# A new timetable for a fused Mamba and MoE layer: where the conv taps, the transposed B and the output projections stand

## The reference

```python
def layer(x):                       # x: 8 x 1024 x 256, fp32
    x = x + mamba(layernorm(x))
    return x + moe(layernorm(x))

def mamba(x):                       # ED = 512 channels, N = 16 states, R = 64
    xp, z = split(x @ in_proj_w.T)
    xc = silu(causal_conv(xp, conv_w, taps=4))          # per channel
    dt, B, C = split(xc @ x_proj_w.T)                   # 64, 16, 16
    delta = softplus(dt @ dt_proj_w.T + dt_proj_b)
    h[t] = exp(delta[t] * A) * h[t-1] + delta[t] * B[t] * xc[t]     # 512 x 16 states
    y = sum_n(h * C) + D * xc
    return (y * silu(z)) @ out_proj_w.T

def moe(x):                         # squared-relu expert; routed experts weigh in by trunc(softmax(top 2))
    return relu(x @ Ws1)**2 @ Ws2 + routed(x)
```

## Time and profile before

| | |
|---|---|
| median of 3 runs | 1702.7 us (1702.11 to 1709.6) |
| the profiled execution | 1708.5 us, its span 1706.6 us |
| busy: DVE, PE, POOL, ACT | 1546.8, 1474.5, 1373.7, 1260.4 us |
| scans (L851), 1024 of them | 613.4 and 582.6 us busy |
| products by C on POOL (L1120), 512 | 1207.4 us busy |
| DMAs of a chunk, 512 KB, median from issue to landing | x 3.8 to 3.9 us, out 2.9 us |

### The profile page before, as it was taken

How to read it: one execution, slowest core, us unless ns; L and a number is a source line. 1 busy time by engine, 2 the same in 40 slices (tenths; PEclk the granted TensorE clock), 3 DMA queues, 4 the chain that set the end, 5 groups by cost and what they waited for, 6 DMA issues and landing times.

```text
span 1706.6 us, 38017 instructions
## 1 busy us (share of the span) xinstructions
PE 1474.5 (86%) x15138; PEld 1129.3 (66%) x15138; DVE 1546.8 (91%) x1833; ACT 1260.4 (74%) x2053; POOL 1373.7 (80%) x991
## 2 busy tenths in 40 slices
PE   7788989888899888988889988898989888898776
PEld 4556666666766666766666766666667666667665
DVE  4888999999999999999999899999989989998885
ACT  5877677887777778787777877788677777777651
POOL 1788788887879788897888878888787987879783
PEclk9999999999999999999999999999999999999999
DMA  4103021130302203031030301203031120302101
GB/s 141 61 2 124 1 100 51 39 113 2 124 26 79 73 14 137 2 112 38 39 112 2 137 13 70 82 15 137 2 112 39 39 99 2 113 25 87 64 14 39
DMA packets 45863, 105.89 MB, mean 62 GB/s; under 512 B 9649, under 2 KB 35121, under 8 KB 37490
## 3 DMA queue, kind: packets, MB, share of 16 engines
q1 hardware_dynamic: 45682, 103.42, 17.2%
HBM read 86.10 MB, written 17.30 MB: 61 GB/s over the span
## 4 chain that ended last, share of the span: by engine, by line
DVE 34%; PE 31%; ACT 18%; issue 13%; POOL 1%; DVEq 1%; SPq 1%; DMA 0%; ACTq 0%; POOLq 0%
DVE hs L851 29%; ACT da L542 10%; PE BX L215 10%; PE PA L257 4%; PE Y L237 4%; PE PA L282 2%; DVE PA L881 2%; PE PB L330 2%; PE PB L282 1%; PE PB L305 1%; PE PB L347 1%; ACT xp L575 1%; PE PA L291 1%; ACT xc L646 1%; PE PB L339 1%
## 5 line engine op out<-in xcount | busy, mean ns | idle before, releaser
L1120 POOL TENSOR_TENSOR hs<-hs,cb 128x1024 f32<-128x1024 f32 x512 | 1207.4, 2365 | 183.3 <-DVE hs L851 162.0
L542 ACT ACTIVATE da<-delta,a_neg 128x512 f32<-128x512 f32 x1024 | 667.6, 711 | 83.4 <-DVE hs L851 82.4
L851 DVE TENSOR_TENSOR_SCAN hs<-da,hlast,BX 128x512 f32<-128x512 f32 x512 | 613.4, 1261 | 56.5 <-PE BX L215 55.6
L851 DVE TENSOR_TENSOR_SCAN hs<-da,BX 128x512 f32<-128x512 f32 x512 | 582.6, 1201 | 52.1 <-PE BX L215 51.0
L237 PEld LDWEIGHTS Y<-ident,hs 128*128 128x128 f32 x4096 | 471.3, 142 | 98.1 <-issue 71.0
L237 PE MATMUL Y<-ident,hs 128*128 128x128 f32 x4096 | 523.8, 275 | 5.4 <-POOL hs L1120 5.3
L215 PE MATMUL BX<-bd,uT 32*128 32x128 f32 x8192 | 302.9, 284 | 155.0 <-DVE hs L851 152.6
L215 PEld LDWEIGHTS BX<-bd,uT 32*128 32x128 f32 x8192 | 253.7, 187 | 214.0 <-DVE hs L851 208.1
L575 ACT ACTIVATE xp<-PA 128x512 f32<-128x512 f32 x60 | 35.9, 598 | 125.9 <-PE PA L257 125.9
L257 PE MATMUL PA<-xnT,w_in 128*128 128x512 f32 x240 | 120.8, 626 | 4.2 <-ACT gate L600 3.4
L1116 POOL COPY hlast<-hs 128x2 f32<-128x2 f32 x256 | 47.9, 187 | 90.2 <-DVE hs L851 90.0
(11 more groups left out here) (169 smaller groups left out, 1467.2 us busy)
## 6 DMA issues: line engine op xcount, KB each, us to landing
cb<-c_scratch SPq DMA_DIRECT2D x64, 1024.0 KB, 4.6
x<-in_x SPq DMA_DIRECT2D x16, 512.0 KB, 3.8
x_scratch<-x2T SPq DMA_DIRECT2D x16, 512.0 KB, 2.6
xt<-in_x SPq DMA_DIRECT2D x15, 512.0 KB, 3.9
out<-x SPq DMA_DIRECT2D x15, 512.0 KB, 2.9
w_in<-in_in_wT SPq DMA_DIRECT2D x1, 1024.0 KB, 10.3
c_scratch<-dbc SPq DMA_DIRECT2D x64, 8.0 KB, 1.5
x2n<-in_x SPq DMA_DIRECT2D x1, 512.0 KB, 4.9
```

Of the source, the lines that this page charges most:

```text
L542: e.activation(da[:, k % DR, q, :], delta[:, g, :], ACT.Exp, scale=a_neg[:, g, n:n + 1]).then_inc(s_da, 1)
L851: e.tensor_tensor_scan(hs[:, k % HR, q, :], da[:, k % DR, q, :], BX[:, :].rearrange("p (t n) -> p n t", n=RT)[:, n % RT, :], hlast[:, g, n ...
L1120: e.tensor_tensor(hs[:, k % HR, :, :], hs[:, k % HR, :, :], cb[:, Q * p:Q * p + Q, :], ALU.mult).then_inc(s_hc, 1)
```

## The change

All five orders and the two bank tables are rewritten. The conv of chunk c+1 begins with group 0 at step 28 of chunk c-1 and goes on at steps 0, 4 and 8; its taps on VectorE are split over odd steps 29/31, 1, 5/7 and 9/11. `act_bt` copies the transposed B from PA to a new SBUF tile `bt`, and `dve_bd` reads it there; the four bd stand at steps 21, 23, 23 and 25. `pe_out` computes tiles in halves, and the second residual tile pair goes through PA. `pe_z(3)` moves to step 1 of the next chunk, `pe_dt(2)` to 8, `pe_ut` and `pe_yt` move, `pool_rstd2` to step 18, `sp_x` to step 6. Waits and semaphores follow the new banks. What is computed stays. The diff, with the removed lines of the orders left out:

```diff
@@ -14,12 +14,12 @@
 EXPS = "natural_log_exp_and_others"
 
 
-BANK_A = {0: [("xp", 1, 0)], 2: [("trc", 2, 1)], 3: [("o", -2, 1)], 4: [("xp", 1, 1)], 7: [("z", 1, 0)],
-          8: [("xp", 1, 2)], 12: [("xp", 1, 3)], 16: [("dbc", 1, 0)], 20: [("bt", 1, 0)], 24: [("z", 1, 2)],
-          26: [("ut", 1, 0)], 28: [("yt", 0, 0)], 29: [("yt", 0, 1)], 30: [("z", 1, 3)]}
-BANK_B = {1: [("trc", 2, 0)], 2: [("o", -2, 0)], 4: [("ut", 0, 1)], 5: [("yt", -1, 3)], 6: [("dt", 0, 2)],
-          9: [("ut", 0, 2)], 10: [("res", -1, 0)], 14: [("res", -1, 1)], 16: [("dt", 0, 3)], 19: [("ut", 0, 3)],
-          20: [("dt", 1, 0)], 22: [("z", 1, 1), ("otr", -1, 0)], 23: [("otr", -1, 1)], 24: [("hl", -1, 0), ("trc0", 2, 0)],
+BANK_A = {0: [("xp0", 1, 0), ("xp", 1, 1)], 2: [("o", -2, 0)], 4: [("xp0", 1, 1), ("xp", 1, 2)],
+          8: [("xp0", 1, 2), ("xp", 1, 3)], 12: [("xp0", 1, 3), ("ut", 0, 2)], 13: [("res", -1, 1)], 16: [("dbc", 1, 0)],
+          20: [("bt", 1, 0), ("yt", 0, 0)], 22: [("z", 1, 1)], 24: [("z", 1, 2)], 26: [("ut", 1, 0)], 27: [("yt", 0, 1)], 28: [("xp", 2, 0)]}
+BANK_B = {1: [("z", 0, 3)], 2: [("ut", 0, 1)], 3: [("o", -2, 1)], 4: [("trc", 2, 0)], 5: [("trc", 2, 1)], 6: [("yt", -1, 3)],
+          7: [("z", 1, 0)], 8: [("dt", 0, 2)], 10: [("res", -1, 0)], 16: [("dt", 0, 3)], 19: [("ut", 0, 3)],
+          20: [("dt", 1, 0)], 22: [("otr", -1, 0)], 23: [("otr", -1, 1)], 24: [("hl", -1, 0), ("trc0", 2, 0)],
           26: [("hl", -1, 1), ("trc0", 2, 1)], 28: [("ht", -1, 0)], 29: [("yt", 0, 2)], 30: [("dt", 1, 1)]}
 
 
@@ -29,10 +29,13 @@
     for c in range(n_chunks):
         for s in range(steps):
             for stage, off, i in places.get(s, ()):
-                if stage in ("trc", "trc0"):
-                    if (stage == "trc0") != (c == 0):
-                        continue
-                    stage = "trc"
+                if stage in ("trc", "trc0") and (stage == "trc0") != (c == 0):
+                    continue
+                if stage in ("xp", "xp0") and (stage == "xp0") != (c == 0) and (c, off) != (0, 2):
+                    continue
+                if (stage, c + off) == ("z", 0):
+                    continue
+                stage = stage.rstrip("0")
                 if 0 <= c + off < n_chunks and (stage, c + off, i) not in at:
                     at[stage, c + off, i] = len(at)
...
@@ -321,16 +325,18 @@
                 mm = e.transpose(bank[:, t * P:(t + 1) * P], gate[c % 2][:, t, g * P:(g + 1) * P], ident[:, :])
             mm.then_inc(done, 1)
 
-        def pe_out(e, c, t, part=0):
+        def pe_out(e, c, t, lo=0, hi=G):
             kk, t2 = divmod(t, 2)
-            if t2 == 0:
-                e.wait_ge(s_pb_out, max(b_use["res", c, kk], b_use["yt", c, G - 1] + 1))
+            bank, n, done, out = bank_of("res", c, kk)
+            if t2 == 0 and lo == 0:
+                e.wait_ge(out, n)
+                e.wait_ge(s_pb_out, b_use["yt", c, G - 1] + 1)
                 e.wait_ge(s_pa_out, a_use["yt", c, 1] + 1)
-            for g in range(part * G // 2, G if part or t != 1 else G // 2):
-                mm = e.matmul(PB[:, t2 * DM:(t2 + 1) * DM], ygT[:, g, t * P:(t + 1) * P], w_out[:, g, :],
+            for g in range(lo, hi):
+                mm = e.matmul(bank[:, t2 * DM:(t2 + 1) * DM], ygT[:, g, t * P:(t + 1) * P], w_out[:, g, :],
                               start=(g == 0), stop=(g == G - 1))
-            if t == 3 or part:
-                mm.then_inc(s_pb, 1)
+            if t2 and hi == G:
+                mm.then_inc(done, 1)
...
@@ -410,71 +416,78 @@
             for c in range(NQ):
                 for s in range(S):
                     k = S * c + s
+                    if on(c):
+                        if s == 2:
+                            pe_ut(e, c, 1)
+                        if s == 8:
+                            pe_dt(e, c, 2)
+                        if s == 16:
+                            pe_dt(e, c, 3)
+                        if s % NP == 2:
+                            pe_skip(e, c, s // NP)
+                    if c == 0 and s in (0, 4, 8, 12):
+                        pe_xp(e, 1, s // 4)
+                    if c and on(c + 1) and s in (0, 4, 8):
+                        pe_xp(e, c + 1, s // 4 + 1)
+                    if s == 12:
+                        pe_ut(e, c, 2)
+                    if s == 28 and on(c - 1):
+                        pe_htr(e, c - 1)
+                    if s == 28 and on(c + 2):
+                        pe_xp(e, c + 2, 0)
+                    if s == 1 and c:
+                        pe_z(e, c, 3)
+                    if s in (2, 3) and on(c - 2):
+                        pe_shared(e, c - 2, s - 2)
+                    if s in (4, 5) and c and on(c + 2):
+                        pe_trc(e, c + 2, s - 4)
+                    if s in (24, 26) and c == 0:
+                        pe_trc(e, 2, s // 2 - 12)
+                    if on(c - 1):
+                        if s == 6:
+                            pe_yt(e, c - 1, 3)
+                        if s == 10:
+                            pe_out(e, c - 1, 0)
+                        if s == 11:
+                            pe_out(e, c - 1, 1, 0, G // 2)
+                        if s == 12:
+                            pe_out(e, c - 1, 1, G // 2, G)
+                        if s == 13:
+                            pe_out(e, c - 1, 2, 0, G // 2)
+                        if s == 14:
+                            pe_out(e, c - 1, 2, G // 2, G)
+                        if s == 15:
+                            pe_out(e, c - 1, 3)
+                        if s == 23:
+                            pe_otr(e, c - 1, 1)
+                        if s in (24, 26):
+                            pe_hidden(e, c - 1, s // 2 - 12)
                     if on(c + 1):
                         if s in (16, 18):
                             pe_dbc(e, c + 1, s // 2 - 8)
                         if s == 20:
                             pe_bt(e, c + 1)
                             pe_dt(e, c + 1, 0)
+                        if s == 7:
+                            pe_z(e, c + 1, 0)
+                        if s in (22, 24):
+                            pe_z(e, c + 1, s // 2 - 10)
                         if s == 26:
                             pe_ut(e, c + 1, 0)
                         if s == 30:
                             pe_dt(e, c + 1, 1)
                     if s == 22 and on(c - 1):
                         pe_otr(e, c - 1, 0)
+                    if s == 19:
+                        pe_ut(e, c, 3)
+                    if s == 20:
+                        pe_yt(e, c, 0)
+                    if k >= 2:
+                        pe_sum(e, k - 2)
+                    if s == 27:
+                        pe_yt(e, c, 1)
+                    if s == 29:
+                        pe_yt(e, c, 2)
                     if s % 2 and 0 <= k + 1 < S * NQ:
                         pe_bx(e, (k + 1) // 2)
...
+        def act_bt(e, c):
+            e.wait_ge(s_pa, a_use["bt", c, 0] + 1)
+            e.wait_ge(s_bd, NR * c)
+            e.activation(bt[:, :, :], PA[:, 0:J * FX].rearrange("p (j f) -> p j f", j=J)[:, :, R:R + N],
+                         ACT.Copy).then_inc(s_pa_out, 1)
...
@@ -732,83 +755,87 @@
             for c in range(NQ):
                 for s in range(S):
                     k = S * c + s
+                    if c == 0 and s == 0:
+                        act_halo(e, 1)
+                    if c == 0 and s in (0, 4, 8, 12):
+                        act_xp(e, 1, s // 4)
+                    if c and on(c + 1) and s in (0, 4):
+                        act_xp(e, c + 1, s // 4 + 1)
+                    if s == 2:
                         act_ut(e, c, 1)
+                    if s == 3:
+                        act_silu_z(e, c)
+                    if s in (4, 5) and c and on(c + 2):
+                        act_trc(e, c + 2, s - 4)
+                    if s == 6 and on(c - 1):
+                        act_yt(e, c - 1, 3)
+                    if s == 8:
+                        act_softplus(e, c, 2)
+                        if c and on(c + 1):
+                            act_xp(e, c + 1, 3)
+                    if s == 12:
+                        act_ut(e, c, 2)
+                    if s == 16:
+                        act_softplus(e, c, 3)
+                    if s == 20 and on(c + 1):
+                        act_bt(e, c + 1)
+                        act_softplus(e, c + 1, 0)
+                    if s == 21 and on(c - 1):
+                        act_norm2(e, c - 1)
+                    if s == 22 and on(c + 1):
+                        act_z(e, c + 1, 1)
+                    if s in (22, 23) and on(c - 1):
+                        act_otr(e, c - 1, s - 22)
+                    if s == 28:
+                        act_yt(e, c, 1)
+                    if s == 28 and on(c - 1):
+                        act_htr(e, c - 1)
+                    if s == 28 and on(c + 2):
+                        act_halo(e, c + 2)
```

(93 more changed lines are left out.)

192 lines of the change are left out of this document (23 added, 169 removed).

## The result

| | before | after |
|---|---|---|
| median of 10 runs | 1704.6 us (1701.9 to 1709.9) | 1717.1 us (1711.2 to 1720.6) |
| ratio, 95% interval | | 1.0065 (1.0047 to 1.0082) |
| the profiled execution, its span | 1708.5, 1706.6 us | 1711.2, 1709.3 us |

The kernel became slower: by 12.5 us between the medians, by 0.65% in the ratio. The forecast was 1713 us, 10.2 us more than the 1702.7 us from which it was reckoned. The two profiled executions lie only 2.7 us apart: that of before is 3.9 us above its median, that of after is the fastest of its ten.

A forecast was written before the change was run, and what follows sets the result against it. VectorE's four-scan groups alternate with TensorE's refill of BX, each gap costing the larger of 1.30 us and its filler. -45.8 - 6.6 + 9 (clock) + 52.6 (lock) + 1 (lateness) = +10.2 us: 1713 us, range 1683 to 1742.

The forecast's parts named there:

- Timetable: VectorE's gaps between scan groups, chunks 2 to 13: new fillers save 7.6 us per two chunks, -45.8 us.
- the small terms: Chunk 1 -4.5, chunk 14 -3.6, chunk 0 +1.4, chunk 15 -0.6, first delta +0.75; together -6.6 us.
- Step 5: Gap after step 5: two taps, 1.40 us, with ScalarE's evacuations ahead of its exps.
- Chunk 0: Taps still at steps 1, 5, 9, 13, delta and stats added to two of them: +1.4 us.
- The start: First delta, before the loop, now stands behind act_bt: +0.75 us.
- The lock of bd: Steps 21 to 25: bd, now with two SBUF inputs, waits for GpSimd's instruction; +2.55 even, +4.6 odd chunks, 52.6 us.
- The clock: TensorE at steps 0 and 1, after idling at 30 and 31: six low-clock stretches of 1.5 us, +9 us.
- no lock: Rival at dve_bd: bd is not held up, prob was slow for another reason; 1664 us, chance 0.17.
- half the lock: Rival at dve_bd: lock holds but costs half, by kinder phases or bd(2) following at once; 1687 us, chance 0.13.
- the harsher phases: Rival: odd-chunk bd phases everywhere and clock falling every chunk at steps 0 and 1; 1741 us, chance 0.23.
- `act_xp` late at step 28: Rival on ScalarE: act_xp(0) behind yt and htr misses its tap by 0.5 us, 14 chunks; 1720 us, chance 0.05.
- The wait for BX: VectorE's wait for TensorE's refill of BX falls from 106.6 us to some 20 to 30 us.

The follow-up runs named there:

- experiment 2: Kernel after without the copy of B: all four bd read PA in PSUM after step 21, pe_yt(0) at step 23; 1694.7 us, ratio 0.9941 to before.
- experiment 10: Kernel after without the copy, bd split after steps 21 and 23, pe_ut(2) of chunk 0, silu of z and act_trc reordered; 1661.1 us, ratio 0.9748 to before.
- experiment 7: Kernel after with the first act_trc ahead of act_xp in ScalarE's order at step 4; 1705.1 us, ratio 0.9999 to before.
- experiment 5: Kernel after with pe_ut(2) of chunk 0 moved from step 12 to step 14, behind the sum; 1712.6 us, ratio 1.0044 to before.
- Experiment 3: Kernel after with bd(3) ahead of dve_top in the gap of step 25; 1707.7 us, ratio 1.0018 to before.
- experiment 6: Kernel after with the silu of z on ScalarE moved from step 3 to step 9; 1712.1 us, ratio 1.0046 to before.

## Why the prediction was right

The forecast was a sum with terms of both signs; here is each by its own numbers.

- **Timetable, forecast -52.4 us with the small terms: right in size.** The gaps after steps 1, 3, 7, 9, 11, 13, 15, 17, 29 measured 2.14, 1.69, 1.30, 1.30, 1.94, 1.46, 1.39, 1.57 and 1.34 us, within 0.15 of the forecast, on the whole 0.3 us less per chunk, -4 us over chunks 2 to 13. Experiments 2 and 10 show the timetable faster than the old one as soon as bd reads PSUM. In experiment 10 fillers of bd still cost 0.85 us a chunk over the two floors in even ones and 0.58 in odd ones, some 11 us; without them it would stand 54 us below the kernel before by the ratio. It has the mends of chunk 0 and step 5 in it, so this is support for the sum and no measurement of it. (Two slips of the sum changed little: chunk 14's 96.1 less 99.9 is -3.8, not -3.6; and the 1.91 us of idle before step 24 in the earlier trace rows is not the usual case. The gap after step 23 was 1.4 to 1.8 us in eleven chunks and 2.9 to 3.1 in four, chunk 8 among them. The sum went by the whole stretch, which had them all.)
- **Step 5, forecast 1.40: this step failed.** "ScalarE ... does evacuations ahead of its exps ... so it has cover of more than 10 us" was true of the exps and said nothing of the order of evacuations among themselves. +1.06 us in even and +0.83 in odd chunks, 11 us over chunks 2 to 13; experiment 7 gives back 12 by the medians, 11 by the ratios.
- **Chunk 0, forecast +1.4 (and +2.55 for bd): mis-sized.** Measured +5.4, bd's 1.25 in it, so +4.1 against +1.4. I had counted VectorE's fillers there and not that one of TensorE's steps now stands in front of them; experiment 5 takes 4.7 us off that gap. The start, forecast +0.75, came 0.5 us earlier.
- **The lock of bd, forecast 2.65, 2.5 and floor in even chunks, 1.5, 4.0 and 3.0 in odd ones: right.** Measured 2.73, 2.31 and 1.30; 1.33, 3.72 and 2.91. Over the floors that is 2.44 and 4.06 us a chunk, and 1.25 in chunk 0 (1.54 and 2.31): 7 x 2.44 + 1.25 + 7 x 4.06 = 47 us against 52.6. Experiment 3 shows the wait as GpSimd's, experiment 2 that it is gone with an input in PSUM. One row, prob's, carried it: the 0.51 us between the end of GpSimd's product and the end of prob are close to the 0.55 us seen here at each held bd. The Trainium skill's page "SBUF — State Buffer", section "SBUF: two separate sides", has the same rule, an exclusive lock for a whole instruction; this case's trace agrees, in both directions.
- **The clock, forecast +9 at steps 0 and 1: the number of stretches was near, the place and the price were wrong.** The gap after step 1 is 2.14 us in every chunk from 1 to 14, so nothing was lost there. The low level came elsewhere: in each odd chunk from 1 to 11 at step 25, behind the held bd(3), and in chunk 13 at step 28. TensorE in chunk 9, and the granted clock:

```profile
1052.46 1.17 PE L219 MATMUL BX<-bd,uT 32*128 32x128 f32 x32 [2.74 <-DVE hs L877]
...
1054.47 2.02 PE L353 MATMUL PB<-w_hr,x2T 128*128 128x136 f32 x8
...
1060.14 1.17 PE L219 MATMUL BX<-bd,uT 32*128 32x128 f32 x32 [0.73 <-DVE hs L877]
1053.60:1056.90 3.30, 3.30 (x19) 3.30 (x16) 3.30 (x3) 0.55 (x2) 3.15 (x5) 0.50 0.31 67
```

  And in chunk 13:

```profile
1462.63 1.09 PE L353 MATMUL PB<-w_hr,x2T 128*128 128x136 f32 x8
...
1468.73 1.17 PE L219 MATMUL BX<-bd,uT 32*128 32x128 f32 x32 [2.38 <-DVE hs L877]
1470.64 3.25 PE L261 MATMUL PA<-xnT,w_in 128*128 128x512 f32 x4
1469.90:1477.30 7.40, 7.28 (x61) 5.08 (x60) 6.35 (x7) 3.97 (x8) 6.00 (x4) 0.77 0.36 144
```

  In both, TensorE stood 2.74 us behind step 25. In chunk 9 it then ran at 1.2 GHz instead of 2.4 (clock 0.50, `pe_hidden` 2.02 us instead of 1.09), but it had time in hand: it was still 0.73 us early at the next BX, and no gap grew. In chunk 13 the clock held, so TensorE was done sooner, stood 2.38 us, and fell to the low level with `pe_xp`, which has no slack: 3.25 us instead of 1.98, and the gap after step 29 is 2.48 us instead of 1.34. So a stretch at the low clock cost nothing six times and 1.1 us once. In experiment 6 it stood at step 28 in three chunks (9, 11, 13), with a gap of 2.48 or 2.49 us each.

  The mean clock alone does not tell the time: in experiment 5 the profiled execution has 0.974 and is the fastest of its five, with six of its low stretches at step 25. The other nine executions of the kernel after have 0.973 to 0.979, at the median 0.977, against 0.981 in the profiled one: 2 x 0.004 x 1716 = 14 us more at the low level, up to 7 us lost if all of it is on the path, and low stretches at step 28 in all seven odd chunks would cost 8 us. The profiled execution is 5.9 us below the median. That agrees in size, but no trace of those executions shows where their low stretches fell, so this stays open.

For chunks 2 to 13 the forecast was -45.8 + 9 + 42.9 + 1 = +7.1. Measured: +1.3, the difference being -4 (gaps), +11 (step 5), -4 (lock), -8 (clock) and -1. So two terms of about 10 us, one missed and one that this execution hardly paid, cancelled; with chunk 0 and the slower usual execution the median came out 2 us from the forecast in the difference. The total is better than its parts, and that closeness is luck.

Of the rivals, no lock (1664 us) is excluded by every held bd, half the lock by 47 us; the harsher phases did not come; and `act_xp` late at step 28 is excluded by the gap of 1.34 us after step 29. The wait for BX, forecast 20 to 30 us, is 58.1: 11 us at step 5 of chunks 1 to 14, 13 in chunk 0, 13 in chunk 15, whose gaps have little filler, and 11 at steps 19 and 27, whose filler is shorter than the floor. The last two groups, 24 us, could have been counted beforehand.

## What to carry to other kernels

Before a small operand is copied from PSUM to SBUF to free a bank, see whether it turns its reader into a VectorE instruction with two SBUF inputs in a stretch where GpSimd is busy: here such a copy cost some 50 us, and holding the bank longer, with another tile moved to the other bank, did without it for some 11 us. If it must be so, put such an instruction where GpSimd's operation is about to end or GpSimd has just waited for VectorE, and look again at the phases after every edit. When an order is rewritten, check for each shared bank which evacuation its engine does first, and check the first chunk by itself: its steps are not those of the others.
